# All keys and queries of layer 0 made before its heads, with the openings in a new order

## The reference

```python
# L0: 32 query heads of 16, 8 key/value heads, each for 4 query heads
q, k, v = x @ Wq + bq, ctx @ Wk + bk, ctx @ Wv + bv
p = softmax(q k^T / 4 + mask)
x = layernorm(x + (p v) @ Wo + bo) * gamma + beta
# L1, for i in (1, 2): 16 heads of 128, one extra key and value (bias_k, bias_v)
h = layernorm(x)
x = x + attention(h @ wq + bq, ctx @ wk + bk, ctx @ wv + bv) @ wo + bo
# and an MLP of 2048
x = x + gelu(layernorm(x) @ w1 + b1) @ w2 + b2
```

## Time and profile before

| | us |
|---|---|
| median of three runs | 2519.05 |
| the profiled execution | 2518.05 |
| its span | 2516.2 |
| PE busy | 2315.7 |
| DVE busy | 1408.2 |
| ACT busy | 998.2 |
| POOL busy | 772.7 |
| mean granted clock of TensorE | 0.974 of full |

### The profile page before, as it was taken

One profiled execution on the slowest core, in us unless ns is written; L12 is line 12 of the kernel. 1 busy time (PEld: TensorE's weight loads), 2 busy tenths in 40 slices (PEclk: granted clock), 3 DMA queues, 4 the chain that ended last, 5 costly groups with the idle time before them and its releaser, 6 DMA issues. The chain is left out here.

```text
span 2516.2 us, 36285 instructions
## 1 busy us (share of the span) xinstructions
PE 2315.7 (92%) x13176; PEld 2073.7 (82%) x13176; DVE 1408.2 (56%) x3154; ACT 998.2 (40%) x2191; POOL 772.7 (31%) x846
## 2 busy tenths in 40 slices
PE   5798799999999999998969978999999999999988
PEld 4576698999989898997757667999989899999976
DVE  4687544454565455456538875454545655454564
ACT  2686433342433333343218854243424333243420
POOL 4022414324141413323541322314141413314055
PEclk9899899999999999999989999999999999999999
DMA  5541223232333323234453303233333323233222
GB/s 190 169 146 59 78 82 99 86 103 87 103 101 93 101 77 102 85 101 128 151 155 111 113 30 98 83 97 98 102 95 97 93 77 112 83 93 117 82 68 82
DMA packets 131943, 253.23 MB, mean 101 GB/s; under 512 B 30800, under 2 KB 50288, under 8 KB 130720
## 3 DMA queue, kind: packets, MB, share of 16 engines
q1 hardware_dynamic: 89560, 140.74, 18.3%
q10 hardware_dynamic: 42208, 110.18, 14.4%
HBM read 222.40 MB, written 31.22 MB: 101 GB/s over the span
## 5 line engine op out<-in xcount | busy, mean ns | idle before, releaser
L595 POOL TENSOR_SCALAR wk_hi<-raw 128x512 fp32r<-128x512 f32 (+1 forms) x84 | 52.3, 622 | 897.2 <-DMA raw<-in_wk 744.5
L1261 ACT ACTIVATE probs<-scores,prm 112x376 f32<-112x376 f32 x256 | 147.0, 574 | 341.8 <-DVE prm L1639 341.8
L704 PE MATMUL pj_two<-ctx_hi,wk_hi 128*128 128x376 f32 x716 | 246.4, 344 | 12.8 <-POOL wk_lo L628 6.7
L705 PE MATMUL pj_two<-ctx_lo,wk_hi 128*128 128x376 f32 x716 | 241.8, 338 | 0.0
L706 PE MATMUL pj_two<-ctx_hi,wk_lo 128*128 128x376 f32 x716 | 241.0, 337 | 0.0
L1398 DVE TENSOR_TENSOR rr<-pj_two,rr 128x448 fp32r<-128x448 f32 (+2 forms) x202 | 133.9, 664 | 163.7 <-ACT rr L1061 163.0
L597 POOL TENSOR_TENSOR wb_lo<-raw,wb_hi 128x512 fp32r<-128x512 f32 x152 | 196.4, 1292 | 12.7
L1400 DVE SCALAR_TENSOR_TENSOR k_lo<-pj_two,cur,k_hi 128x375 fp32r<-128x375 f32 x172 | 104.3, 607 | 169.3 <-ACT k_hi L1063 169.3
L1063 ACT ACTIVATE k_hi<-pj_two,cur 128x375 fp32r<-128x375 f32 x172 | 98.6, 573 | 247.1 <-PE pj_two L706 242.2
L704 PE MATMUL pj_two<-pt_hi,nat 125*128 125x448 f32 x462 | 171.9, 372 | 9.4 <-issue 8.9
L709 PE MATMUL tp_two<-ident,probs 112*126 112x112 f32 (+1 forms) x1152 | 161.8, 265 | 13.0 <-DVE probs L1647 7.2
(11 more groups left out here) (239 smaller groups left out, 6648.3 us busy)
## 6 DMA issues: line engine op xcount, KB each, us to landing
nat<-nat_scratch ACTq DMA_DIRECT2D x256, 384.0 KB, 3.7
raw<-in_wk SPq DMA_DIRECT2D x72, 256.0 KB, 3.7
raw<-in_wq SPq DMA_DIRECT2D x72, 256.0 KB, 3.3
raw<-in_wo SPq DMA_DIRECT2D x72, 256.0 KB, 2.6
raw<-in_wv SPq DMA_DIRECT2D x64, 256.0 KB, 4.3
raw<-in_w SPq DMA_DIRECT2D x64, 256.0 KB, 2.9
nat_scratch<-rr SPq DMA_DIRECT2D x8, 1536.0 KB, 7.0
queries_scratch<-rr SPq DMA_DIRECT2D x32, 224.0 KB
```

The costliest lines, as they stand in the source:

```text
L595: nc.gpsimd.tensor_scalar(hi, src, 1.0, 0.0, ALU.mult, ALU.add).then_inc(split_hi, 1)
L704: nc.tensor.matmul(dst, l_hi, r_hi, start=first, stop=False)
L705: nc.tensor.matmul(dst, l_hi, r_lo, start=False, stop=False)
L1261: nc.scalar.activation(probs[0:L, h, 0:SK], scores[n % SCR][0:L, 0:SK], ACT.Exp, bias=neg_max[0:L, h:h + 1], accum_out=row_sum[0:L, h:h + ...
```

## The change

All keys and queries of L0 are made in the openings, none between the heads (`L0_AT` is gone). The order of the openings is new. SyncE loads Wk0 as half rows into both slots at once, Wq0 by column blocks (one per chunk), the tokens before Wv0, and the mask before the queries are stored. Natural context has three places, the third in the tile of Wo; ScalarE's queue issues its stores. Queries are stored once instead of twice and read back by four DMAs per batch. GpSimd clears all of `qo` (VectorE cleared the empty half before), clears the third place and makes the extra value rows, which VectorE did. VectorE does `out0` one head later.

```diff
 def pre_units(half):
-    names = natural_units(half, 0) + [("k", 0)] + [("q", 0), ("k", 1)] * half + [("vt", 0)]
...
+    if half == 0:
+        order = "n0 n1 k0 k1 n2 n3 q0 k2 vt0 k3 vt1 v0 q1 vt2 v1 q2 vt3 v2 q3 v3"
+    else:
+        order = "k0 q0 k1 vt0 q1 vt1 v0 k2 q2 vt2 v1 k3 q3 vt3 v2 v3"
...
-L0_AT = {1: ("k", 2), 5: ("k", 3), 12: ("q", 1), 44: ("q", 2), 76: ("q", 3)}
...
+NAT_AT = [[0, 1, 2, 0], [0, 1, 0, 1]]
...
-        q0_split = [rr[:, at_q0 + e * T:at_q0 + (e + 1) * T] for e in range(2)]
+        q0_split = [[rr[:, at_q0 + e * T:at_q0 + (e + 1) * T] for e in range(2)]] + [
+            [t[:].rearrange("p h n -> p (h n)")[:, c * T:(c + 1) * T] for t in (pt_hi, pt_lo)] for c in range(C0 - 1)]
...
-        stage = [rr[:, i * NAT:(i + 1) * NAT] for i in range(2)]
+        stage = [rr[:, 0:NAT], rr[:, NAT:2 * NAT], flat_o[:, 0:NAT]]
```

SyncE's list (parameters and the bias of keys come from other places now):

```diff
-                load_rows(base, wk0, 0, 0)
+                for i in range(2):
+                    sp.wait_ge(raw_free[i], base // 2 + 1)
+                    for j in range(2):
+                        rows = wk0[(2 * i + j) * P:(2 * i + j + 1) * P, 0:GW].rearrange("p (c r n) -> p c r n", c=C0, r=2)
+                        sp.dma_start(raw[:, i, 2 * P * j:2 * P * (j + 1)].rearrange("p (c n) -> p c n", c=C0),
+                                     rows[:, :, 0, :]).then_inc(raw_ready[i], 16)
+                if hf == 0:
+                    sp.dma_start(prm, prm_in).then_inc(setup_dma, 16)
...
+                load_q0(base + RAW_Q0, 0)
+                for c in range(DC - 1):
+                    load_x(c)
+                if hf == 0:
+                    store_keys0(0, *pre_split("k", 0))
+                load_x(DC - 1)
+                if hf == 0:
...
+                    store_keys0(1, *pre_split("k", 1))
...
+                load_v0(0)
+                load_v0(1)
+                if hf == 0:
+                    load_keys0(0, 0)
+                    load_keys0(0, 1)
+
+                    sp.wait_ge(pj_free, pre_freed("n", 2, SC - 1) + PJ)
+                load_mask()
+                load_q0(base + RAW_Q, 1)
+                if hf == 1:
+                    store_keys0(0, *pre_split("k", 0))
+                store_queries0(0, *pre_split("q", 0))
+                load_q0(base + RAW_Q + 1, 2)
+                if hf == 1:
+                    load_keys0(0, 0)
+                    store_keys0(1, *pre_split("k", 1))
+                load_queries0(0, 0)
+                load_q0(base + RAW_Q + 2, 3)
+                if hf == 1:
+                    load_keys0(0, 1)
+                    store_queries0(1, *pre_split("q", 1))
+                for b in (2, 3):
+                    store_keys0(b, *pre_split("k", b))
+                    if hf == 1:
+                        store_queries0(b, *pre_split("q", b))
+                    load_queries0(0, b - 1)
+                    load_keys0(0, b)
+                load_queries0(0, HB - 1)
+                if hf == 0:
...
+                    for c in range(1, C0):
+                        store_queries0(c, *pre_split("q", c))
...
+                        sp.dma_start(bx_dram[:, r, :].rearrange("g (h n) -> g h n", h=HPG)[:, :, 0:P],
...
                 for c in range(1, C0):
-                    store_queries0(c, *aux_split("q", c))
                     for b in range(HB):
                         load_keys0(c, b)
                         load_queries0(c, b)
```

GpSimd, ScalarE and VectorE:

```diff
+            nc.gpsimd.memset(stage[2].bitcast(F32), 0.0).then_inc(setup_pool, 1)
...
+                if hf == 1:
+
+                    pool.wait_ge(pj_ready, PJ_AT[0]["end"])
+
+                nc.gpsimd.memset(qo[:].bitcast(F32), 0.0).then_inc(rows_empty, 1)
+                values0(base + RAW_V, use_k + 1)
+                for c in range(1, C0):
+                    queries0(base + RAW_Q + c - 1, c, use_b)
+                if hf == 0:
+                    extra_values()
...
-            act.wait_ge(setup_dma, 80)
...
+                    if hf == 0 and name == ("k", 2):
+                        store_nat0(2)
+                    if hf == 0 and name == ("v", 0):
+                        store_nat0(3)
...
+                    if n == 1:
+
+                        for t in q0_out:
+                            act.wait_ge(t, (hf + 1) * 32)
...
+                    if n >= 17 and n % 8 == 1:
+                        out0((n - 17) // 8)
...
-                    if n >= 16 and n % 8 == 0:
-                        out0((n - 16) // 8)
```

More of the change, by code:

```diff
@@ L61, in pre_units @@
 def pre_units(half):
-    names = natural_units(half, 0) + [("k", 0)] + [("q", 0), ("k", 1)] * half + [("vt", 0)]
[L63 to L67, removed]
+    if half == 0:
+        order = "n0 n1 k0 k1 n2 n3 q0 k2 vt0 k3 vt1 v0 q1 vt2 v1 q2 vt3 v2 q3 v3"
+    else:
+        order = "k0 q0 k1 vt0 q1 vt1 v0 k2 q2 vt2 v1 k3 q3 vt3 v2 v3"
+    names = []
+    for name in order.split():
+        kind, i = name[:-1], int(name[-1])
+        names += natural_units(half, i) if kind == "n" else [(kind, i)]
     return names
@@ L339, in xattn_program @@
         ctx_copied = sem("ctx_copied")
-        nat_out = [sem("nat_out0"), sem("nat_out1")]
+        nat_out = [sem(f"nat_out{i}") for i in range(3)]
         nat_in = [sem(f"nat_in{c}") for c in range(DC)]
@@ L1106, in natural @@
             def natural(half, b, base):
-                if b > 1:
-                    act.wait_ge(nat_out[b % 2], (half * HB // 2 + b // 2) * 16)
+                place, before = NAT_AT[half][b], NAT_N[half][b]
+                if before > 0:
+                    act.wait_ge(nat_out[place], before * 16)
+                elif place < 2:
+                    act.wait_ge(stage_rows, place + 1)
+                else:
+                    act.wait_ge(setup_pool, 5)
                 for s in range(SC):
-                    move(stage_parts[b % 2][0:KC, :, 0, s, :],
+                    move(stage_parts[place][0:KC, :, 0, s, :],
                          pj[(base + s) % PJ][0:KC, :].rearrange("p (c n) -> p c n", c=DC),
@@ L1116, in load_ctx, with store_nat @@
                 act.dma_start(came[0][b], ctx_t[:, b, :].rearrange("(c p) n -> p c n", p=P)).then_inc(ctx_in[b], 16)
+            def store_nat(half, b, freed):
+                act.wait_ge(pj_free, freed + PJ)
+                place = NAT_AT[half][b]
+                act.dma_start(nat_dram[half * HB + b], stage[place].bitcast(F32)).then_inc(nat_out[place], 16)
             load_ctx(0)
             load_ctx(1)
+            for c in range(C0):
+                at = PRM_C + 4 + 3 * ((c - 1) % C0)
+                bias0 = prm_in[0:KV2 * 2 * HD0, at:at + 1].rearrange("(k e d) n -> k e d n", k=KV2, e=2)[:, 0, :, :]
+                act.dma_start(bk0[32 * c:32 * c + 32, :], bias0, allow_slow_non_contiguous=True).then_inc(setup_dma, 16)
             for n in "bk":
@@ L1153, in keys0 @@
                         act.wait_ge(k0_out[b % 2], (hf * 2 + b // 2) * 64)
+                    if hf == 0 and b == 0:
+                        act.wait_ge(setup_dve, 1)
                     move(k0_split[b % 2][0], bank[:, 0:SK], ready, n, bias=bk0, mid=mid)
                 def queries0(c, bank, ready, n, mid):
-                    if hf * C0 + c > 0:
-                        act.wait_ge(q0_out, (hf * C0 + c) * 64)
                     bias = PRM_C + (0 if c == 0 else 3 * c)
-                    move(q0_split[0], bank[:, 0:T], ready, n, bias=prm[:, bias:bias + 1], mid=mid)
+                    move(q0_split[c][0], bank[:, 0:T], ready, n, bias=prm[:, bias:bias + 1], mid=mid)
                     if c == C0 - 1:
@@ L1462, in natural @@
                 for s in range(SC):
-                    hi, lo = (stage_parts[b % 2][0:KC, :, e, s, :] for e in range(2))
+                    hi, lo = (stage_parts[NAT_AT[half][b]][0:KC, :, e, s, :] for e in range(2))
                     lo_of(lo, pj[(base + s) % PJ][0:KC, :].rearrange("p (c n) -> p c n", c=DC), hi, pj_mid,
@@ L1472, in split_ctx @@
                       ctx_hi_ready, half * HB + b + 1, ctx_ready)
[L1475 removed]
+            nc.vector.memset(stage[0][96:P, :].bitcast(F32), 0.0).then_inc(stage_rows, 1)
             dve.wait_ge(setup_pool, 2)
```

284 lines of the change are left out of this document (115 added, 169 removed).

## The result

The changed kernel took 2504.05 us (median of five runs, 2497.39 to 2506.21), the kernel before 2519.05 beside it (five runs, 2516.07 to 2525.37): ratio 0.9925, 95% interval 0.9908 to 0.9942. It is faster, as forecast, but outside the range of 2454 to 2492. The profiled execution took 2500.87 us with a span of 2499.0 (2518.05 and 2516.2 before), so 17.2 us of span are to be found, and 29.8 of the forecast's 47 are missing.

What follows compares the result with a forecast made beforehand. TensorE was busy 92% of the span, with three engines nearly full between heads. Gains of 15 + 17.1 + 0.4 + 14.5 = 47 us took 2518 to 2471; range 2458 to 2484, with most of two neighbours 2454 to 2492.

Steps and rivals of the forecast that it cites:

- Loops: Between heads, both halves: five units taken out, load_q(0) no longer late, out0 moved; gains of 17.1 and 14.5 us.
- opening 0: Start of half 0 up to its head loop: effective start 64 for 78.9, 15 us gained, bounds 4 and 21.
- the last store is issued at 61 and lands at 64: SyncE's list in half 0's opening: last query store out at 61, shifting the loop by 4 us, to 61.5.
- Wv0 at 32, before vt0: hidden: GpSimd in half 0's opening: token splits done at 25.5, clear of qo at 29, Wv0 at 32, costing nothing.
- I add 2.5 us: Half 0's opening: allowance for nearly full DMA queues, 19.5 MB to move, giving an effective start of 64.
- Opening 1: Start of half 1: first maximum at 1320.6 for 1321.0, gain 0.4 us, bounds 6 lost and 5 gained.
- four issues of some 0.5 us: MLP: natural stores move from SP to ScalarE's queue, costing nothing, or 2 us if not covered.
- One queue in series: Rival, 0.04: openings' 18 landings each delay the next step; slower from 2.6 us more per landing, 2543 at 4 us.
- Full DMA engines: Rival, 0.13: first maximum stays at 74 to 79, only the loops gain, time 2486.
- What would show it: Signs: first maxima about 64 and 1288, loops some 131 us, mask issued near 28, ScalarE's query-store wait some 3 us.
- loops over 137 us: Sign of being wrong, between heads: a loop lasting over 137 us, where some 131 us was expected.
- the second opening over 43: Sign of being wrong, half 1: over 43 us from end of k0 to first maximum, 37 us before.

Runs made afterwards that it cites:

- q_bx_early: Changed kernel with half 0's stores of queries 1 to 3 and the bias rows' DMAs moved ahead of the last loads in SyncE's list: 2491.05 us.
- no_nat: Changed kernel with half 0's four natural stores cut to 64 KB each, the full bytes written behind head 4: 2496.2 us.
- nat_times: Changed kernel with half 1's natural stores spread again, batches 0 to 2 ahead of MLP gelus, batch 3 behind unit v1 of the opening: 2500.38 us.
- nat_q0: Changed kernel with q_bx_early and nat_times, half 0's batch 2 natural store behind head 4, half 1's key/query stores ahead of reloads, batch 3's store behind q0: 2482.93 us.
- nat_q0_cut: nat_q0 with half 0's natural stores of batches 0, 1 and 3 cut to 64 KB, full bytes written behind head 4: 2478.04 us.

## Why the prediction was wrong

**Loops: right.** 16.7 and 14.2 us for 17.1 and 14.5. The units taken out and the late load_q(0) were the excess: GpSimd no longer waits for a load in the loop, and from the third on the eights are 8.27 to 8.32. The count-back helps: what the first two eights lost (14.0 and 0.8 us in half 0, 1.1 and 1.1 in half 1) stands under the openings.

**The step that failed** is in opening 0: "the last store is issued at 61 and lands at 64". It was issued at 82.4 and its buffer was free at 89.1. The sum over SyncE's list counted what each row takes to issue (2.9 us for keys, 3.2 for loads, 1.5 for a query), and not that between two rows the list stands until a landing comes back. Of the 21.4 us, 8.5 were there when the queries 0 were stored (44.5 for 36); from there the list took 37.9 us for 25, and stood 11.2 of them for landings (7.9, 1.3 and 2.0). Moving three ready stores out from behind these waits, in q_bx_early, gave 9 us.

A second step failed beside it: "Wv0 at 32, before vt0: hidden". In the changed kernel TensorE waited for Wv0's split until 45.6, 3.8 us.

**A mis-sized term:** "I add 2.5 us" for contention. no_nat shows 8.8 us at the first maximum and 13.5 at the last. The forecast had worked out that 19.5 MB must pass, and from that the average looked bearable. But GpSimd has two raw slots, so each late landing of 224 KB holds the tokens' split (11.5 us of waits, in three), and TensorE behind it. An average over the opening doesn't show such a wait.

**Opening 1:** first maximum expected 39.0 us after the MLP, came at 45.9. The forecast feared the mask; the output landed in 6.1 us (8.8 in the earlier trace rows), and the mask left at 1281.35, 10.0 us after the MLP's end, as it had (9.8). It counted moving the natural stores as "four issues of some 0.5 us" and left out where their 1.5 MB land. nat_times shows that part, 7.9 us, and nat_q0 shows that it pays only if the store isn't put onto the query stores instead. The wait at head 1, small in the changed kernel (1317.2 to 1326.5, 9.3 for an eight), is mostly hidden by the late opening: ScalarE waited 3.1 us there. The forecast had priced it for half 0 and not at all for half 1.

**The rivals.** "One queue in series" had the mechanism (each landing is what the next step waits for) with a price of 2.6 us per landing to lose everything. 29.8 us over its 18 landings is 1.7 each. It and the forecast are ends of one scale, and the truth lay between them, above the range's end at 2492 where no rival stood. "Full DMA engines" put the first maximum at 74 to 79 (it came at 70) and missed head 1. Its rate of 268 GB/s is what flowed from 20 to 60 us (265 and 274), but only 159 flowed from 60 to 80, so full engines may be part of the late landings and are not all of them.

**What would show it:** the mask left at 42.2, not 28; ScalarE's wait at head 1 was 16.3 us, not 3; of the tests for being wrong, loops over 137 us and the second opening over 43 both came true (146.1 in half 0; 43.8 from the end of k0), and the first maximum stayed under 72.

## What to carry to other kernels

Price an in-order queue by walking it: for each entry the later of "its turn" and "its data", plus the landing wherever the next entry waits for it. A transfer's latency beside big stores on another queue is not its latency alone, and with two slots the split behind it waits too. When work is moved into a stretch whose end is set by several transfers, the wait named last hides the others: shorten one and look who is second before counting the gain.

## What the runs showed of the hardware

- A load of 224 KB landed in 3.2 us, and in 8.3 beside a 1.5 MB store on the other queue, though the mean rate over the six microseconds was about the same (234 and 247 GB/s). The latency more than doubled at nearly equal throughput; the DMA engines' busy share was 0.77 and 0.92.
- Issuing itself slows: four key stores took SyncE 2.4 to 2.7 us at best and 5.8 with the 1.5 MB store issued beside them, and everything behind in the list left later by it. Without that store they took 3.7 and 4.1.
- Six query stores of 224 KB issued on another engine's queue in half 0 freed their buffer no earlier (80.1 and 79.3 us).
- Two of GpSimd's four token subtractions in nat_q0_cut took 2.5 and 2.6 us, the others 1.1. Each began 0.1 to 0.2 us into a VectorE subtraction of two SBUF operands that took 1.7 (21.27 and 24.70). The forecast had this at 1.15 us each from the earlier trace rows; it was 1.4.
